# First attention: three PSUM banks for the second scores and two for the first, in place of two and three

## The chip, the cores and the metric

The kernel runs on one core of one Trainium2 chip, as one launch. The metric is the device time of that launch in microseconds; lower is better. The core has five engines with a queue of instructions each: TensorE (matmuls, written PE below, its weight loads PEld), VectorE (DVE), ScalarE (ACT), GpSimd (POOL) and SyncE (SP), which here issues DMAs.

## The reference

Four layers over x of shape 32 x 256 x 128 (batches, tokens, width), each followed by a residual addition and a layernorm without weights:

```
x = layernorm(x + attention0(x))   # 16 heads of 8, rotary embedding, softmax(q k / sqrt(8)) v, then w_out and bias
x = layernorm(x + ffn0(x))         # ternary weights, gelu, layernorm inside
x = layernorm(x + attention1(x))   # queries are the keys, heads mixed after the softmax
x = layernorm(x + ffn1(x))         # silu(gate) * up, integer weights
```

The change touches attention0 alone. There, for each of the 32 batches and 16 heads, 256 x 256 scores are computed, the maximum of each query's row is subtracted, the exponential is taken, and the result is multiplied with the values and divided by its sum.

## The kernel before

All four layers are phases of one program, written out engine by engine; `program` (L1720 on) lists what each engine does in which order, and semaphores tie the engines together. In the first attention one call of `step(i, on)` is a pass: it works on several batches at once, each at another stage. The 16 positions s = 0 to 15 of a pass are its inner loop, on every engine. `on(k)` tells whether batch i+k exists. Passes run from i = -4 to n+1 with n = 32; those from 4 to 27 are the body of a hardware loop, the others are written out.

Each score is computed twice. The *first scores* (`first_score`, L1114) are those of batch i+1: two matmuls, one for each half of 128 queries, write a 128 x 512 bank. VectorE reads that bank with one `tensor_reduce` (`max_of_head`, L967) to get the negated maximum of each row. Eight heads' maxima are turned by TensorE (`shifts_turned`, L1038), copied to SBUF by ScalarE (`shift_rows_out`) and sent by DMA into a row of the query operand, so that the *second scores* come out with the maximum already subtracted. The second scores (`second_score`, L1101) are those of batch i, with keys on the partitions. ScalarE reads their bank with one `Exp` (L912) into `probs`. `products_by_group` (L1047) multiplies four heads' `probs` with the values, after positions 3, 7, 11 and 15.

In `both_scores` (L1128) TensorE interleaves the two kinds, tile by tile: second, first, second, first. The first and second scores of one position use different rows of the array. TensorE takes its instructions in the order written, so whatever it waits for also holds up what stands behind.

Ahead of the scores of a position, `others_of_first` (L1160) puts TensorE's other work: at 2 the projection of V for batch i+1, a turn of maxima and one projection (k side) for batch i+3; at 6 two kinds of transposes (`heads_t`, `x_in`); at 10 a turn of maxima and the transposes of `o`; at 14 the output projection and the other projection (q side) for batch i+4. VectorE and ScalarE have the matching work at fixed positions among their maxima and exps: VectorE has a rotation (`rotate`, L979, 128 x 512) after the maximum of position 2 and one before that of position 15, a reciprocal before that of 6, scalings after those of 6 and 7, and an addition (y) after that of 14.

PSUM has eight banks. In the first attention the first scores have banks 0 to 2, the second scores banks 3 and 4, the products bank 5, and all other work banks 6 and 7. The banks are taken in a fixed order, and the order repeats with each pass of 16 positions:

```
s1_order = (0, 1, 2) * 4 + (0, 1) * 2     # bank of the first scores at position s
s2[s % 2]                                 # bank of the second scores at position s
```

Before the first tile of a position, `first_score` waits until the maximum that read this bank last is done (semaphore `max_done`; `s1_free`, L563, counts how many positions ago that was), and `second_score` waits on `exp_done` for the exp two positions back. With the order above the first scores wait for the maximum three positions back at positions 3 to 13, seven back at 2, and two back at 14, 15, 0 and 1.

The second attention is built by the same function with other banks: two for each kind of score, both taken in turn.

Of the kernel before, what the change touches and what calls it, by code (L numbers as in the profile page):

```python
# [9 lines left out]
ACT = mybir.ActivationFunctionType  # L10
AX = mybir.AxisListType

P = 128
D = 128
TOK = 256
TILES = TOK // P
HEADS = 16
# [16 lines left out]
RING = 8  # L34
# [46 lines left out]
def wait(eng, sem, count):  # L81

    if isinstance(count, int) and count <= 0:
        return
    eng.wait_ge(sem, count)
# [18 lines left out]
class Phase:  # L104
# [8 lines left out]
    def sem(self, name):  # L113
        self.sems[name] = self.core.sem(f"{name}_{self.name}")
        return self.sems[name]
# [23 lines left out]
def times(i, k, n):  # L139

    if isinstance(i.half, int):
        return max(0, min(n, 2 * i.half + i.odd + k + 1))
    assert i.first + i.odd + k >= 0, "no wait in a loop is for less than one"
    return i.half * 2 + (i.odd + k + 1)
# [303 lines left out]
def attention(nc, core, layer, banks, scratch, ctx, x_dram=None, before=None):  # L448
# [9 lines left out]
    n = core.n  # L458
    first = layer == 0
# [2 lines left out]
    half_heads = HEADS // 2  # L462

    b = [core.bank[k] for k in banks]
    s1, s2 = (b[0:3], b[3:5]) if first else (b[0:2], b[2:4])
    pv, m0, m1 = (b[5:6], b[6], b[7]) if first else (b[4:7], b[7], b[7])
    s1_order = (0, 1, 2) * 4 + (0, 1) * 2 if first else (0, 1) * 8
    groups = HEADS // 4
    regions = groups // 2
    slots = Slots(first)  # L470
# [3 lines left out]
    def sb(name, shape, dt=FP32):  # L474
        return ctx.enter_context(nc.sbuf_tensor(f"{name}_{layer}", shape, dt))
# [12 lines left out]
    probs = sb("probs", [P, RING, TILES, TOK])  # L488
# [42 lines left out]
    max_done = sem("max_done")  # L531
# [4 lines left out]
    exp_done = sem("exp_done")  # L536
# [23 lines left out]
    def s1_bank(s):  # L560
        return s1[s1_order[s]]

    def s1_free(b, s):  # L563

        ago = min(k for k in range(1, HEADS + 1) if s1_order[(s - k) % HEADS] == s1_order[s])
        return b.number() * HEADS + (s - ago + 1)

    banked = [h for h in range(HEADS) if h != BESIDE]
# [9 lines left out]
    def stack_rows(parity, rows=HEAD_ROWS):  # L578
        return slice(parity * TILE_ROWS, parity * TILE_ROWS + rows)
# [234 lines left out]
    def _(act):  # L814
        def shift_rows_out(b, hf):

            act.wait_ge(shifts_in_psum, b.number() * 2 + (hf + 1))

            wait(act, shifted[hf], b.number() * 16)
            act.activation(shift_rows[hf][:, :], m0[:, :].bitcast(BF16)[0:half_heads, SHIFTS_AT:SHIFTS_AT + TOK], ACT.Copy).then_inc(shift_rows_ready, 1)  # L820

        def take_heads(b, r):

            act.wait_ge(pv_done, b.number() * groups + 2 * (r + 1))
            act.activation(heads_t[b.odd][:, r, :], pv[0][:, 0:TOK], ACT.Copy).then_inc(pv_taken, 1)
# [15 lines left out]
        def norm(b, ts=range(TILES)):  # L841

            act.wait_ge(rstd_ready, b.number() + 1)
            act.wait_ge(norm_shift_ready, b.number() + 1)
            for t in ts:
                act.activation(core.x_all[:, b.number(), t, :], y_of(b)[:, t, :], ACT.Identity, scale=rstd[:, t:t + 1],
                               bias=norm_shift[:, t:t + 1]).then_inc(x_ready, 1)
# [10 lines left out]
        def second_part(b):  # L858

            act.wait_ge(rest_ready, times(b, 0, n))  # L860
            act.activation(parts[b.odd][:, 1, 0, :], rest[:, 0, :], ACT.Copy).then_inc(part1_ready, 1)

        def step(i, on):
            for s in range(HEADS):
                if not first and s == 4 and on(slots.q_ahead):
                    second_part(i.plus(slots.q_ahead))
                if first and s == slots.shifts1 and on(0):
                    shift_rows_out(i, 1)
                if s == 4 and first and on(-1):
                    take_heads(i.plus(-1), 1)  # L870
                if first and s == slots.norm and on(-2):
                    norm(i.plus(-2), (0,))
                if first and s == slots.v + 2 and on(1):
                    b = i.plus(1)
                    act.wait_ge(v_in_psum, times(i, 1, n))

                    wait(act, pv_done, times(i, -1, n) * groups)
                    act.activation(values[b.odd][:, :, :, 0:HD],
                                   m0[:, 0:TOK].rearrange("p (t h d) -> p t h d", t=TILES, d=HD),
                                   ACT.Copy).then_inc(v_taken, 1)  # L880
                if not first and s == 15 and on(slots.v_ahead):
                    act.wait_ge(v_in_psum, times(i, slots.v_ahead, n))

                    wait(act, values_ready, times(i, 1, n) * (2 * TILES))
                    act.activation(v_in[:, :, :].rearrange("p t d -> p (t d)"), m0[:, TOK:2 * TOK], ACT.Copy).then_inc(v_taken, 1)
                if s == 13 and first and on(0):
                    take_heads(i, 0)
                if s == slots.ot + (1 if first else 0) and on(-1):
                    act.wait_ge(ot_in_psum, times(i, -1, n))
                    act.activation(o_t[:, :], m1[:, 0:TOK], ACT.Copy).then_inc(ot_ready, 1)  # L890
                if s == slots.shifts0 and on(1):
                    shift_rows_out(i.plus(1), 0)
                if s == slots.xt + (1 if first else 0) and on(slots.xt_ahead):
                    b = i.plus(slots.xt_ahead)
                    act.wait_ge(xt_in_psum, times(i, slots.xt_ahead, n))

                    if first:
                        wait(act, x_v_ready, times(i, 2, n))
                        act.activation(x_t[b.odd][:, :], m0[:, 0:TOK], ACT.Copy).then_inc(xt_ready, 1)  # L899
                    else:  # L900
                        act.activation(x_t[b.odd][:, :], m1[:, 0:TOK], ACT.Identity, scale=core.cols[:, 8:9],
                                       bias=core.cols[:, 9:10]).then_inc(xt_ready, 1)
                if not first and s % 2 and on(0 if s > 4 else -1):
                    scale_head(i if s > 4 else i.plus(-1), (s - 4) % HEADS)
                if on(0):
                    act.wait_ge(s_in_psum, i.number() * HEADS + (s + 1))

                    if first and s % 4 == 0:
                        wait(act, pv_done, i.number() * groups + (s // 4 - 1))
                    if not first:  # L910
                        wait(act, pv_done, i.number() * HEADS + (s + 1 - RING))
                    act.activation(probs[:, s % RING, :, :].rearrange("p t n -> p (t n)"), s2[s % 2][:, :], ACT.Exp,  # L912
                                   scale=scale).then_inc(exp_done, 1)
                if not first and s == slots.shifts1 and on(0):
                    shift_rows_out(i, 1)
                if not first and s == slots.q and on(slots.q_ahead):
                    take_qk(i.plus(slots.q_ahead))
                if first and s == HEADS - 1 and on(-2):
                    norm(i.plus(-2), (1,))
                if not first and s == slots.norm and on(-1):  # L920
                    norm(i.plus(-1))
# [115 lines left out]
    def _(pe):  # L1037
# [63 lines left out]
        def second_score(b, s, t):  # L1101

            if t == 0:
                if s % half_heads == 0:
                    pe.wait_ge(shifted[s // half_heads], b.number() * 16 + 16)

                wait(pe, exp_done, b.number() * HEADS + (s - 1))
            rows = stack_rows(s % 2, HEAD_ROWS + 1)
            score = pe.matmul(s2[s % 2][:, t * TOK:(t + 1) * TOK], core.k_stack[b.odd][rows, s // 2, t * P:(t + 1) * P],  # L1109
                              core.q_stack[b.odd][rows, s // 2, :], start=True, stop=True)  # L1110
            if t == TILES - 1:
                score.then_inc(s_in_psum, 1)

        def first_score(b, s, t):  # L1114

            if t == 0:
                if s % half_heads == 0:
                    pe.wait_ge(stacked[s // half_heads], b.number() * (16 * reads) + 16 * reads)

                wait(pe, max_done, s1_free(b, s))  # L1120
            h = s ^ 1
            rows = stack_rows(h % 2)
            score = pe.matmul(s1_bank(s)[:, t * TOK:(t + 1) * TOK], core.q_stack[b.odd][rows, h // 2, t * P:(t + 1) * P],  # L1123
                              core.k_stack[b.odd][rows, h // 2, :], start=True, stop=True)
            if t == TILES - 1:
                score.then_inc(max_in_psum, 1)
# [758 lines left out]
```

## Time and profile before

| | |
|---|---|
| time, median of 3 runs | 1529.43 us (1526.62 to 1534.0) |
| time of the profiled execution | 1530.18 us |
| its span in the profile | 1527.9 us |
| busy share of the span: PE, PEld | 95%, 75% |
| busy share of the span: DVE, ACT, POOL | 77%, 69%, 63% |
| mean granted TensorE clock | 0.976 of full speed |
| instructions | 55309 |

The span is the time from the first to the last record of the profiled execution; the time beside it includes what lies around it. The first attention takes from about 37 us (its first scores) to about 500 us, where the feed-forward layer's work is mixed in. In a profile, busy time is the union of an engine's instructions. Matmuls are pipelined: one starts 0.1 us after another though each is 0.27 us long, so their starts say more than their durations. The list of waits names, for each idle stretch of an engine, the instruction whose semaphore came last; in a list in order of time, equal instructions in a row are merged (x16 is a count), and a gap with its releaser stands in square brackets.

### The profile page before, as it was taken

Reading aid. Unit: us, or ns where it says so; the run is one execution under the profiler, and the core shown is the slowest. Engines: PE = TensorE matmul, PEld = TensorE weight load, DVE = VectorE, ACT = ScalarE, POOL = GpSimd, SP = SyncE. Lnnn points to the kernel's source line nnn. Section 1 sums busy time; section 2 is a strip of 40 time slices with the busy share of each in tenths; the row PEclk is TensorE's granted clock in tenths of the full one; section 3 lists DMA queues with packets and bytes.
Section 4 is the critical chain, followed back from the end, with each engine's and each line's share of the span. In section 5 each row is a group of like instructions: output and inputs, shape, how many; then the busy total and the mean of one; then the engine's idle time right before and its main releaser. Section 6 shows DMA issues by size and latency. Waiting matters only on the chain. (4 is left out here: it accounts for less than half of the span.)

```text
span 1527.9 us, 55309 instructions
## 1 busy us (share of the span) xinstructions
PE 1456.4 (95%) x17642; PEld 1141.6 (75%) x17642; DVE 1180.8 (77%) x3338; ACT 1056.9 (69%) x2581; POOL 967.4 (63%) x1160
## 2 busy tenths in 40 slices
PE   5999999999999899979999999999999999998998
PEld 3445555554554499959989999999999999897997
DVE  4688888888888478878887888788878887864666
ACT  2477777777778888856777777777777777773332
POOL 4465565656554167777777877787778777852222
PEclk7699999999999999979999999999999999999999
DMA  5345454454444100122222222222222222201211
GB/s 146 105 128 135 132 140 128 132 140 126 134 131 135 34 32 33 55 74 79 82 69 90 76 79 69 90 76 80 69 90 76 80 70 85 75 23 32 65 62 52
DMA packets 174124, 133.93 MB, mean 88 GB/s; under 512 B 13787, under 2 KB 145126, under 8 KB 174054
## 3 DMA queue, kind: packets, MB, share of 16 engines
q1 hardware_dynamic: 172944, 132.37, 30.0%
q8 instruction: 40, 0.66, 0.2%
q10 hardware_dynamic: 1110, 0.66, 0.1%
q14 instruction: 30, 0.25, 0.1%
HBM read 64.82 MB, written 55.05 MB: 78 GB/s over the span
## 5 line engine op out<-in xcount | busy, mean ns | idle before, releaser
L971 DVE TENSOR_REDUCE shifts<-bank 128x2 bf16<-128x512 f32 x1024 | 682.2, 686 | 158.7 <-PE bank L1123 158.1
L912 ACT ACTIVATE probs<-bank 128x512 f32<-128x512 f32 x1024 | 579.9, 595 | 120.1 <-PE bank L1109 116.3
L1071 PE MATMUL bank<-values,probs 64*128 64x129 f32 x8192 | 577.8, 276 | 0.9 <-DVE o_even L938 0.7
L1071 PEld LDWEIGHTS bank<-values,probs 64*128 64x128 f32 x8192 | 528.8, 188 | 20.4 <-issue 4.5
L1123 PE MATMUL bank<-stack 48*128 48x256 bf16 x2048 | 373.3, 277 | 29.7 <-DVE shifts L971 24.1
L1109 PE MATMUL bank<-stack 49*128 49x256 bf16 x2048 | 373.3, 274 | 7.6 <-ACT probs L912 2.4
L715 POOL TENSOR_TENSOR values<-mix,v_in 128x1024 f32<-128x1024 f32 x128 | 302.3, 2363 | 0.0
L1109 PEld LDWEIGHTS bank<-stack 49*128 49x128 bf16 x2048 | 163.9, 95 | 139.4 <-ACT probs L912 89.7
L724 POOL TENSOR_TENSOR o_odd<-o_odd,scaled 128x256 f32<-128x256 f32 x224 | 163.5, 730 | 128.0 <-ACT scaled L838 124.3
L838 ACT ACTIVATE scaled<-bank,recips 128x128 f32<-128x128 f32 x448 | 138.6, 360 | 92.8 <-DVE recips L965 92.7
L1123 PEld LDWEIGHTS bank<-stack 48*128 48x128 bf16 x2048 | 156.2, 96 | 54.0 <-DVE shifts L971 37.8
L938 DVE SCALAR_TENSOR_TENSOR o_even<-bank,recips,o_even 128x128 f32<-128x128 f32 x448 | 136.6, 347 | 7.9
L1061 PE MATMUL bank<-probs,values 128*32 128x256 f32 x2048 | 138.8, 389 | 0.0
L965 DVE RECIPROCAL recips<-bank 128x2 f32<-128x2 f32 x512 | 84.4, 165 | 58.0 <-PE bank L1071 48.9
L740 POOL TENSOR_TENSOR shifted_var<-moments,ln_shift 128x2 f32<-128x2 f32 x64 | 12.6, 196 | 156.0 <-DVE moments L1021 145.6
L1061 PEld LDWEIGHTS bank<-probs,values 128*32 128x32 f32 x2048 | 53.8, 110 | 50.1 <-issue 28.4
L793 POOL TENSOR_TENSOR exact<-turned 128x512 f32<-128x512 f32 x32 | 40.6, 1268 | 76.2 <-DVE turned L979 71.5
L1228 PE MATMUL bank<-x_t,w_qk 128*128 128x256 f32 x256 | 76.0, 424 | 1.4 <-ACT x_t L899 1.4
L1524 PE MATMUL bank<-w_proj,h_t_f 128*128 128x129 f32 x512 | 70.2, 281 | 2.3 <-issue 1.4
L1617 POOL TENSOR_TENSOR var_f<-moments_f,ln_shift 128x2 f32<-128x2 f32 x32 | 6.2, 195 | 102.3 <-DVE moments_f L1675 102.3
L1524 PEld LDWEIGHTS bank<-w_proj,h_t_f 128*128 128x128 f32 x512 | 63.5, 191 | 5.9 <-issue 4.1
L1639 ACT ACTIVATE gate_f<-bank 128x256 f32<-128x256 f32 x96 | 36.6, 383 | 43.1 <-PE bank L1697 43.0
(165 smaller groups left out, 2176.8 us busy)
## 6 DMA issues: line engine op xcount, KB each, us to landing
stack<-score_parts SPq DMA_DIRECT2D x64, 512.0 KB, 4.2
stack<-score_parts SPq DMA_DIRECT2D x256, 96.0 KB
score_parts<-parts SPq DMA_DIRECT2D x256, 64.0 KB, 2.1
score_parts<-parts SPq DMA_DIRECT2D x128, 96.0 KB, 2.6
score_parts<-parts SPq DMA_DIRECT2D x64, 192.0 KB, 2.3
x_in_f<-x_all SPq DMA_DIRECT2D x64, 128.0 KB, 2.0
score_parts<-parts SPq DMA_DIRECT2D x64, 128.0 KB, 2.2
x_in<-in_L_attn_x SPq DMA_DIRECT2D x32, 128.0 KB, 2.1
```

Of the source, the lines that this page charges most:

```text
L715: pool.tensor_tensor(values[i.plus(1).odd][:, t, heads, 0:D], core.mix[:, heads, :], v_in[:, t, :].unsqueeze(1).broadcast_to([P, half_head ...
L724: pool.tensor_tensor(o_odd[b.odd][:, :, :], o_odd[b.odd][:, :, :], scaled[:, h // 2 % 4, :, :], op=ALU.add).then_inc(odd_added, 1)
L838: act.activation(to, pv_bank(h)[:, t * (D + 1):t * (D + 1) + D], ACT.Copy, scale=recips[:, h % 2, t:t + 1]).then_inc(scaled_ready, 1)
L912: act.activation(probs[:, s % RING, :, :].rearrange("p t n -> p (t n)"), s2[s % 2][:, :], ACT.Exp, scale=scale).then_inc(exp_done, 1)
L938: dve.scalar_tensor_tensor(o_even[b.odd][:, t, :], part, recips[:, h % 2, t:t + 1], o_even[b.odd][:, t, :], op0=ALU.mult, op1=ALU.add).the ...
L965: dve.reciprocal(recips[:, h % 2, :], sums).then_inc(recips_ready, 1)
L971: dve.tensor_reduce(shifts[:, :, hf, col], s1_bank(s)[:, :].rearrange("p (t n) -> p t n", t=TILES), op=ALU.max, axis=AX.X, negate=True).th ...
L1061: last = pe.matmul(pv[0][VW * a:VW * (a + 1), 0:TOK], values[b.odd][:, t, :, :].rearrange("p h c -> p (h c)")[:, start:start + VW], probs[ ...
L1071: return pe.matmul(pv_bank(h)[:, q * (D + 1):(q + 1) * (D + 1)], probs[rows, h % RING, t, q * P:(q + 1) * P], values[b.odd][rows, t, h, :] ...
L1109: score = pe.matmul(s2[s % 2][:, t * TOK:(t + 1) * TOK], core.k_stack[b.odd][rows, s // 2, t * P:(t + 1) * P], core.q_stack[b.odd][rows, s ...
L1123: score = pe.matmul(s1_bank(s)[:, t * TOK:(t + 1) * TOK], core.q_stack[b.odd][rows, h // 2, t * P:(t + 1) * P], core.k_stack[b.odd][rows, ...
L1524: pe.matmul(out_banks[i.odd][:, t * width:t * width + D + 1], h_t[i.odd][:, c, own], core.w0_proj[:, c, :], start=(c == 0), stop=(c == chu ...
```

## The change

The first attention's five score banks are split the other way round: banks 0 and 1 for the first scores, banks 2, 3 and 4 for the second. The order of the first scores becomes (0, 1) eight times, so each waits for the maximum two positions back. The second scores take their three banks in turn, the last position taking the second of them; they wait for the exp three positions back at positions 3 to 14, four back at 0 and 2, two back at 1 and 15. The counting function is now used for both. The second attention's banks and waits stay the same. No instruction is added, removed or moved.

```diff
-    s1, s2 = (b[0:3], b[3:5]) if first else (b[0:2], b[2:4])
+    s1, s2 = (b[0:2], b[2:5]) if first else (b[0:2], b[2:4])
     pv, m0, m1 = (b[5:6], b[6], b[7]) if first else (b[4:7], b[7], b[7])
-    s1_order = (0, 1, 2) * 4 + (0, 1) * 2 if first else (0, 1) * 8
+    s1_order = (0, 1) * 8
+    s2_order = (0, 1, 2) * 5 + (1,) if first else (0, 1) * 8
...
-    def s1_free(b, s):
-
-        ago = min(k for k in range(1, HEADS + 1) if s1_order[(s - k) % HEADS] == s1_order[s])
+    def bank_free(b, s, order=s1_order):
+
+        ago = min(k for k in range(1, HEADS + 1) if order[(s - k) % HEADS] == order[s])
         return b.number() * HEADS + (s - ago + 1)
...
-                    act.activation(probs[:, s % RING, :, :].rearrange("p t n -> p (t n)"), s2[s % 2][:, :], ACT.Exp,
+                    act.activation(probs[:, s % RING, :, :].rearrange("p t n -> p (t n)"), s2[s2_order[s]][:, :], ACT.Exp,
...
-                wait(pe, exp_done, b.number() * HEADS + (s - 1))
+                wait(pe, exp_done, bank_free(b, s, s2_order))
             rows = stack_rows(s % 2, HEAD_ROWS + 1)
-            score = pe.matmul(s2[s % 2][:, t * TOK:(t + 1) * TOK], core.k_stack[b.odd][rows, s // 2, t * P:(t + 1) * P],
+            score = pe.matmul(s2[s2_order[s]][:, t * TOK:(t + 1) * TOK], core.k_stack[b.odd][rows, s // 2, t * P:(t + 1) * P],
...
-                wait(pe, max_done, s1_free(b, s))
+                wait(pe, max_done, bank_free(b, s))
```

## Rows read from the trace of the kernel before

The pass shown runs from position 10 at 300.90 us over position 2 of the next pass (308.32) to position 8 at 315.00. L1109 are second scores, L1123 first scores, L1061 products, L971 maxima, L912 exps.

**Rows 1.** The page's part 1: busy us, share of the span, instructions.
```profile
PE 1456.4 (95%) x17642; PEld 1141.6 (75%) x17642; DVE 1180.8 (77%) x3338; ACT 1056.9 (69%) x2581; POOL 967.4 (63%) x1160
```

**Rows 2.** Stretches: busy us of PE, PEld, DVE, ACT, POOL (count), clock, DMA share, GB/s.
```profile
51.00:67.00 16.00, 15.21 (x101) 6.49 (x101) 9.47 (x17) 7.75 (x17) 7.48 (x7) 0.50 0.47 122
...
200.00:300.00 100.00, 94.43 (x1048) 50.87 (x1047) 84.15 (x177) 76.91 (x169) 57.08 (x75) 1.00 0.50 133
```

**Rows 3.** Groups by line, 150 to 450 us: busy us, mean ns, idle before.
```profile
L971 DVE TENSOR_REDUCE shifts<-bank 128x2 bf16<-128x512 f32 x325 | 211.4, 684 | 46.8 <-PE bank L1123 46.8
L912 ACT ACTIVATE probs<-bank 128x512 f32<-128x512 f32 x325 | 184.7, 596 | 59.3 <-PE bank L1109 58.6
```

**Rows 4.** Waits, 150 to 450 us: us in total, times, longest.
```profile
PEld bank L1109 <- ACT probs L912: 53.2, 163, 0.4
...
PEld bank L1123 <- DVE shifts L971: 19.5, 20, 1.0
...
PE bank L1123 <- DVE shifts L971: 13.9, 20, 0.7
```

**Rows 5.** TensorE in order of time, one pass: start us, us, what, count.
```profile
300.90 0.44 PE L1210 MATMUL bank<-ident,o 128*128 128x128 f32 x2
301.31 0.28 PE L1109 MATMUL bank<-stack 49*128 49x256 bf16 x1
...
301.80 0.28 PE L1109 MATMUL bank<-stack 49*128 49x256 bf16 x1
...
302.20 1.07 PE L1061 MATMUL bank<-probs,values 128*32 128x256 f32 x16
303.20 0.28 PE L1109 MATMUL bank<-stack 49*128 49x256 bf16 x1
...
308.00 0.28 PE L1123 MATMUL bank<-stack 48*128 48x256 bf16 x1 [0.69 <-DVE shifts L971]
...
308.32 0.71 PE L1168 MATMUL bank<-w_v,x_v 128*128 128x128 f32 x4
...
310.23 0.28 PE L1109 MATMUL bank<-stack 49*128 49x256 bf16 x1
...
310.77 1.07 PE L1061 MATMUL bank<-probs,values 128*32 128x256 f32 x16
311.77 0.28 PE L1109 MATMUL bank<-stack 49*128 49x256 bf16 x1
...
312.84 0.38 PE L1198 MATMUL bank<-ident,x_in 128*128 128x128 f32 x2
313.15 0.28 PE L1109 MATMUL bank<-stack 49*128 49x256 bf16 x1
...
313.60 0.28 PE L1109 MATMUL bank<-stack 49*128 49x256 bf16 x1
...
315.00 0.28 PE L1109 MATMUL bank<-stack 49*128 49x256 bf16 x1
```

**Rows 6.** VectorE in order of time, same pass and columns.
```profile
307.25 0.69 DVE L971 TENSOR_REDUCE shifts<-bank 128x2 bf16<-128x512 f32 x1
...
310.69 0.70 DVE L971 TENSOR_REDUCE shifts<-bank 128x2 bf16<-128x512 f32 x1 [1.03 <-PE bank L1123]
311.30 0.68 DVE L979 TENSOR_TENSOR turned<-bank,rope 128x512 f32<-128x512 f32 x1
311.89 1.88 DVE L971 TENSOR_REDUCE shifts<-bank 128x2 bf16<-128x512 f32 x3
...
313.95 0.63 DVE L971 TENSOR_REDUCE shifts<-bank 128x2 bf16<-128x512 f32 x1
```

**Rows 7.** ScalarE in order of time, same pass and columns.
```profile
312.45 1.72 ACT L912 ACTIVATE probs<-bank 128x512 f32<-128x512 f32 x3
```

**Rows 8.** TensorE in order of time, V projection eleven passes on.
```profile
471.64 0.71 PE L1168 MATMUL bank<-w_v,x_v 128*128 128x128 f32 x4
```

## The prediction

> **What bounds the kernel now.** I began with the page's busy shares [rows 1]. They name TensorE at 95%, but for matmuls such a share counts overlapping instructions, so it can't say that TensorE sets the pace. The change touches only the first attention, so I then read that stretch alone [rows 2]: of 100 us VectorE is busy 84, ScalarE 77, and the granted clock is 1.00, the upper level of 2.4 GHz. No engine is full, so the pace is set by a loop of waits. The projection for V starts once per pass, at 308.32 and again at 471.64, eleven passes later [rows 5, 8]: 14.85 us per pass.
>
> Next, the price of one head. A row maximum on VectorE lasts 0.69 us, an exp on ScalarE 0.60 [rows 3]. Back to back their starts are 0.60 and about 0.49 apart: three maxima take 1.88 us, and three exps 1.72, the third waiting a little [rows 6, 7]. TensorE needs about 0.23 for both scores of a head: the two heads 2 and 3 and the switch to other work take 0.54, from 310.23 to 310.77 [rows 5]. So the scores are cheap for TensorE. It stalls because a bank is not yet read.
>
> Then who it waits for [rows 4]. In 300 us, the second scores' weight loads stood 53.2 us behind ScalarE, in 163 places; the first scores stood 19.5 us (loads) and 13.9 us (matmuls) behind VectorE. Taken at face value that asks for a third bank at ScalarE. The order of time says otherwise. At 303.20, where such a wait is booked, TensorE has just finished the products that began at 302.20, and a group of products takes 1.00 wherever it is followed by scores, as from 310.77 to 311.77 [rows 5]. It was working, and the load had nothing to wait for. I count the starts of matmuls instead. Real stalls of one pass, S1(s), S2(s) being the scores at position s, M(s) and E(s) the maximum and the exp that empty them:
> 1. S1(1) waits for M(15), which ends at 307.25 + 0.69 = 307.94; TensorE resumes at 308.00, 0.06 later. The row's gap of 0.69 begins where the matmul before it ended; that lasts 0.27, and the next could have started with it, so the stall is 0.96 [rows 5, 6].
> 2. S2(7) starts 0.45 after S2(6), against 0.23: 0.22 for E(5), which starts about 312.94 and ends 0.60 later [rows 5, 7].
> 3. S2(11) starts 0.49 after S2(10): 0.26 for E(9).
> 4. S2(10) comes about 0.1 late behind E(8): the two transposes at 300.90 need some 0.3 (as the two at 312.84, after which scores start at 313.15), and it starts at 301.31.
>
> **What the change does to each stall.** No instruction is added or moved. Only which earlier reader a score waits for changes. First scores at positions 3 to 13 wait for M(s-2) in place of M(s-3) (position 2 too, from seven back). Second scores wait for E(s-3) or E(s-4), and for E(s-2) at 1 and 15 alone. At 14, 15, 0 and 1 the first scores already wait for two back. So stall 1 stays: M(15) is behind M(14), the addition to y and a rotation on VectorE, a chain that begins with TensorE's own scores at position 14. Stalls 2 to 4 go, worth 0.22 + 0.26 + 0.10 = 0.58 per pass. What is late next, walked on the clock of this pass:
>
> - **Position 5.** M(2) starts 0.46 after the scores of position 2 (310.23, 310.69), then comes the rotation, then M(3) at 311.89 [rows 6]. M(3) ends at 311.89 + 0.69 = 312.58, and S1(5) may go at 312.64. TensorE gets there at 311.77 + 0.23 = 312.00. New stall 0.63. The transposes, with which heads_t and x_in are turned, queue behind it.
> - **Positions 6 and 7.** Position 6 moves from 313.15 to 313.78, and 7 comes 0.23 later at 314.01. E(4) is long done for S2(7), and M(5) ends about 313.78 (the three maxima from 311.89 end at 313.77). So 7 is 0.41 late against 313.60: of 0.63, ScalarE's stall gives 0.22 back. Position 8 comes at 315.00 + 0.41 = 315.41.
> - **Position 9.** M(6) can't start before 313.78 + 0.46 + some 0.03, 314.27 in place of 313.95. M(7) follows after M(6) at 0.60 and a scaling at about 0.18: 315.05, ending 315.74, so S1(9) goes at 315.80. TensorE arrives at 315.41 + 0.23 = 315.64: stall 0.16, now 0.57 late.
> - **Positions 10 and 11.** Without stall 4, position 10 comes 0.47 late. M(8) starts at 315.41 + 0.46 = 315.87, M(9) 0.60 after it, ending 317.16, so S1(11) goes at 317.22. One tile and the switch (0.31) later the products start at 317.53. Before, they started at 302.20 + 14.85 = 317.05. **+0.48.**
> - **Positions 12 to 1.** M(10) and M(11) end at 317.8 and 318.4; the scores that want them come at 318.53 and 318.76. From 14 on the waits are those of before. Everything shifts by 0.48, stall 1 keeps its size.
>
> So 0.63 + 0.16 and some 0.33 at position 11 come in, 0.58 go, and a little is lost to rounding: I take +0.47 per pass. DMAs: none is added, and the shift rows' queue is moved as a whole with its pass.
>
> **The sum.** Passes 1 to 28 have this shape: 28 x 0.47 = 13.2. Passes 29 and 30 have no rotation at position 2 (it is for batch i+3), so M(3) is not late: nothing. Passes -1 and 0 run while the clock is still low (0.50, the level of 1.2 GHz, from 51 to 67 us [rows 2]); first scores alone wait there for VectorE, about one maximum (0.69) more each before the projections: 1.4. The second attention gets the same banks and waits as before: nothing. 1530.2 for the profiled execution, plus 14.6, is 1544.8; the median of the three runs is 0.75 lower, so I say **1544.5**. A measurement of this kernel can tell about 0.5% (7.6 us) from no change.
>
> The bounds per pass: if none of ScalarE's stalls gave anything back, 0.63 + 0.16 + 0.33 = 1.12; if VectorE never held a bank, -0.58. I take 0.47 because each end needs M(3) or E(5) elsewhere than the rows have them.
>
> The Trainium skill speaks on both sides. Its page "Perfetto Trace Analysis", section "Identifying the Most-Contended Engine", ranks VectorE and ScalarE by occupancy and would have the fuller one served first: that is VectorE, from which the change takes a bank, as the trace here bears out. The same page of the Trainium skill, section "Optimization Strategy", says that consistent bubbles can mean too little PSUM; by that, the 163 waits for ScalarE would call for exactly this bank, and the time would come out as in rival A below.
>
> **Rivals.**
> - **A, faster.** The waits booked to ScalarE [rows 4] are real throughout, and M(3) is in time. Place: S1(5). It decides if M(3) ends before 311.94, 0.64 earlier than the row has it. Price: stalls 2 to 4 go and nothing comes, 28 x -0.58 = -16: 1514. For it: the size of the booked waits. Against: the rotation between M(2) and M(3) is in every pass. 6%, with smaller gains.
> - **B, absorbed.** The delay at position 5 is swallowed later, above all by stall 1, so that +0.1 to +0.2 per pass is left: 28 times that, plus 1.4, gives 1534 to 1537. For it: 0.96 us of slack stands there. Against: that stall's chain starts from TensorE's position 14 and moves with it. 9%.
> - **C, no effect.** TensorE's 95% is its true limit and stalls only change places: 1530. Against: 0.96 us of nothing at S1(1) in each pass. 5%.
> - **D, the full price.** VectorE becomes the loop: each of its waits adds (1.12 per pass) and ScalarE's savings don't show, as E(5) and E(8) are late behind the delayed scores. 28 x 1.12 = 31, plus 1.4: 1563. For it: two banks give a round trip of 0.69 + 0.06 + 0.46 = 1.21 for two maxima, exactly their 0.60 each, without slack. Against: outside positions 5, 9 and 11 TensorE's other work comes later than the maxima. 10%.
> - **The forecast**, +0.3 to +0.7 per pass, 1540 to 1551: 70%.
>
> **Numbers.** Slower by over 0.5%: forecast and D, 0.80. Within: B and C, 0.14. Faster: A, 0.06. The range leaves out A, C and most of D: 1534 to 1555, down into B, and up to the forecast's edge with a third of the way to D.
>
> **What would show it.** In the profile after: a pass of 15.3 us by the starts of the V projection; no gap before S2(7) and S2(11), and instead one of about 0.6 before S1(5), 0.2 before S1(9) and 0.3 before S1(11), with VectorE as releaser; waits of first scores for VectorE up by about a us per pass; the 0.69 gap at S1(1) unchanged; the second attention as long as before. The forecast is wrong if the pass is 14.3, if S1(5) starts within 0.3 of S1(4), or if the gap at S1(1) shrinks by what is lost at position 5.

## The result and the profile after

The changed kernel takes 1543.88 us (median of 6 runs, 1540.23 to 1544.83), against 1528.84 for the kernel before (median of 6, 1526.62 to 1534.0): a ratio of 1.0091, 95% interval 1.0073 to 1.011. It is slower by 15 us, and the interval is clear of no change and above the 0.5% named in the prediction. The profiled execution took 1544.36 us, its span 1542.1.

First the length of a pass. Below is TensorE in order of time in the changed kernel, one pass from one V projection (L1169, here one line later than before) to the next; columns as in [rows 5].

```profile
301.98 0.71 PE L1169 MATMUL bank<-w_v,x_v 128*128 128x128 f32 x4
...
303.89 0.28 PE L1110 MATMUL bank<-stack 49*128 49x256 bf16 x1
...
305.44 0.28 PE L1110 MATMUL bank<-stack 49*128 49x256 bf16 x1
...
305.67 0.27 PE L1110 MATMUL bank<-stack 49*128 49x256 bf16 x1
306.30 0.28 PE L1124 MATMUL bank<-stack 48*128 48x256 bf16 x1 [0.36 <-DVE shifts L972]
...
307.43 0.28 PE L1110 MATMUL bank<-stack 49*128 49x256 bf16 x1
...
307.66 0.27 PE L1110 MATMUL bank<-stack 49*128 49x256 bf16 x1
...
307.97 1.07 PE L1062 MATMUL bank<-probs,values 128*32 128x256 f32 x16
308.98 0.28 PE L1110 MATMUL bank<-stack 49*128 49x256 bf16 x1
...
309.21 0.27 PE L1110 MATMUL bank<-stack 49*128 49x256 bf16 x1
309.44 0.28 PE L1124 MATMUL bank<-stack 48*128 48x256 bf16 x1
...
309.97 0.44 PE L1211 MATMUL bank<-ident,o 128*128 128x128 f32 x2
310.34 0.28 PE L1110 MATMUL bank<-stack 49*128 49x256 bf16 x1
...
310.57 0.27 PE L1110 MATMUL bank<-stack 49*128 49x256 bf16 x1
310.84 0.28 PE L1124 MATMUL bank<-stack 48*128 48x256 bf16 x1
...
311.16 1.07 PE L1062 MATMUL bank<-probs,values 128*32 128x256 f32 x16
...
316.95 0.28 PE L1124 MATMUL bank<-stack 48*128 48x256 bf16 x1 [0.69 <-DVE shifts L972]
...
317.27 0.71 PE L1169 MATMUL bank<-w_v,x_v 128*128 128x128 f32 x4
```

A pass is now 317.27 - 301.98 = 15.29 us, against 14.85 [rows 5, 8]. Counted from the V projection: position 2 starts at 1.91, as before (310.23 - 308.32). Position 4 is also where it was, 3.46. Then the first scores of position 5 start at 4.32, with the new gap of 0.36 and VectorE as releaser, and everything behind is late: position 6 at 5.45 (before 4.83), 8 at 7.00 (6.68), 10 at 8.36 (7.84), the products at 9.18 (8.73, which is 302.20 + 14.85 - 308.32). The gap of 0.69 before S1(1), at 316.95, is the one of [rows 5]. The row's 0.36 is the idle time after the last matmul; counted from starts, as in the prediction, S1(5) comes 0.63 after S2(5), at which TensorE had arrived (306.30 - 305.67), S1(9) 0.23 after S2(9) and S1(11) 0.27 after S2(11).

The waits of 150 to 450 us, in the columns of [rows 4]:

```profile
PEld bank L1124 <- DVE shifts L972: 41.6, 79, 1.0
PEld bank L1110 <- ACT probs L913: 33.9, 98, 0.4
...
PE bank L1124 <- DVE shifts L972: 20.4, 39, 0.7
```

The first scores' loads wait 41.6 us for VectorE, in 79 places, where it was 19.5 us in 20 [rows 4]: four per pass (positions 1, 5, 9 and 11) in place of one. The waits booked to ScalarE fell from 53.2 to 33.9. VectorE around position 5, with the columns of [rows 6]:

```profile
304.35 0.70 DVE L972 TENSOR_REDUCE shifts<-bank 128x2 bf16<-128x512 f32 x1 [1.03 <-PE bank L1124]
304.96 0.68 DVE L980 TENSOR_TENSOR turned<-bank,rope 128x512 f32<-128x512 f32 x1
305.56 1.89 DVE L972 TENSOR_REDUCE shifts<-bank 128x2 bf16<-128x512 f32 x3
...
307.89 0.70 DVE L972 TENSOR_REDUCE shifts<-bank 128x2 bf16<-128x512 f32 x1 [0.19 <-PE bank L1124]
...
309.30 0.28 DVE L954 TENSOR_TENSOR o<-bank,recips 128x128 f32<-128x128 f32 x1
309.49 2.60 DVE L972 TENSOR_REDUCE shifts<-bank 128x2 bf16<-128x512 f32 x4
```

M(2) starts 0.46 after the scores of position 2, the rotation follows, M(3) starts at 305.56, and S1(5) goes at 306.30, 0.05 after M(3)'s 0.69 are over. The stretch from 200 to 300 us as in [rows 2]:

```profile
200.00:300.00 100.00, 93.67 (x1037) 49.66 (x1039) 83.39 (x170) 75.80 (x166) 58.40 (x72) 1.00 0.47 126
```

VectorE went from 84.2 to 83.4 and ScalarE from 76.9 to 75.8, at the same granted clock of 1.00 (2.4 GHz): neither reader became busier. The shares fell by 1% and the pass grew by 3%; busy time per pass therefore rose a little, which fits readings that no longer follow one another at once and are booked with their full length (0.69 in place of 0.60 for a maximum).

### The profile page after: what moved, and what is told of

Read it like the earlier page. It is cut to its first block and busy times, and to the rows that moved or that the text cites. A ratio compares the mean times of both kernels' runs of the same rounds, so it can differ in the third digit from the quotient of the medians.

```text
span 1542.1 us, 55297 instructions
## 1 busy us (share of the span) xinstructions
PE 1466.1 (95%) x17642; PEld 1144.9 (74%) x17642; DVE 1188.2 (77%) x3338; ACT 1062.1 (69%) x2581; POOL 967.0 (63%) x1160
## 5 line engine op out<-in xcount | busy, mean ns | idle before, releaser
L1124 PE MATMUL bank<-stack 48*128 48x256 bf16 x2048 | 379.3, 277 | 41.7 <-DVE shifts L972 36.4
L1110 PE MATMUL bank<-stack 49*128 49x256 bf16 x2048 | 377.3, 274 | 2.7 <-ACT probs L913 1.3
```

The costliest lines, as they stand in the source:

```text
L1110: score = pe.matmul(s2[s2_order[s]][:, t * TOK:(t + 1) * TOK], core.k_stack[b.odd][rows, s // 2, t * P:(t + 1) * P], core.q_stack[b.odd][r ...
```

## The experiments

Pass lengths below are differences of successive starts of the V projection, as above; unlike a run's time they repeat to 0.01 or 0.02 us within the hardware loop. The exceptions are e2 and e5, which alternate between two values, and the first or second looped pass of e2, e5, e7 and e9, which is 0.02 to 0.19 longer. The kernel before, run beside the experiments, has medians of 1529.6 to 1530.4. Where the table says "one run", the time is too coarse for small differences (the kernel before spreads over 1524.6 to 1535.2), and the pass decides.

| kernel | pass, us | time, us |
|---|---|---|
| before | 14.85 | 1528.84 |
| the change | 15.29 | 1543.88 |
| e1: two and two banks | 15.29 | 1545.03 |
| e2: before, S1(5) waits two back | 15.17 to 15.22 | 1541.8 (one run) |
| e3: before, S1(9), S1(11) wait two back | 14.94 | 1531.74 (one run) |
| e7: before, half of each exp | 14.35 | 1511.62 (one run) |
| e4: change, rotation behind M(3) | 15.08 | 1537.37 (one run) |
| e5: before, rotation behind M(3) | 14.87 to 14.90 | 1534.23 (one run) |
| e6: before, loop written out | 14.61 | 1521.5 |
| e8: before, q rotation behind M(15) | 14.52 | 1521.23 (one run) |
| e9: before, rotation and y behind M(15) | 14.19 | 1509.29 |
| e10: change, rotation and y behind M(15) | 14.62 | 1528.34 (one run) |
| e11: e9 with the loop written out | 14.02 | 1505.21 |

**Is the third bank of the second scores worth anything?** e1 takes it away again.

```diff
-    s2_order = (0, 1, 2) * 5 + (1,) if first else (0, 1) * 8
+    s2_order = (0, 1) * 8
```

> The changed kernel with the second scores on two banks again, so that the first attention has two and two and one bank lies idle. Theory: the third bank of the second scores buys nothing once the first scores have two, because TensorE now comes to the second scores after the exps: E(9) would end about 8.5 us after the V projection, S1(11) waits until 8.8 anyway. Pass 15.29 us (starts of the V projection), as with the change, time 1542 to 1546. Rival (the third bank gives back the 0.58 us per pass of ScalarE's stalls, as the prediction booked it): pass 15.6 to 15.9, time 1552 to 1560.

Measured: pass 15.29, time 1545.03 (four runs), ratio to before 1.0108 (1.0086 to 1.013). The pass is that of the change to 0.01 us. The rival, that the bank gives back 0.58, is out. TensorE of this kernel at positions 9 and 11:

```profile
308.95 0.28 PE L1110 MATMUL bank<-stack 49*128 49x256 bf16 x1
309.12 0.28 PE L1124 MATMUL bank<-stack 48*128 48x256 bf16 x1
...
310.30 0.28 PE L1110 MATMUL bank<-stack 49*128 49x256 bf16 x1
310.51 0.28 PE L1124 MATMUL bank<-stack 48*128 48x256 bf16 x1
```

S2(9) and S2(11) still stall a little (308.95 and 310.30), but each time the first scores behind them wait longer, until 309.12 and 310.51. TensorE's order is fixed, so only the later of the two releases counts.

**Which positions pay?** e2 and e3 keep the banks of before and make single waits stricter.

```diff
         ago = min(k for k in range(1, HEADS + 1) if s1_order[(s - k) % HEADS] == s1_order[s])
+        if first and s in (5,):
+            ago = 2
```

This is e2; e3 has `(9, 11)` in place of `(5,)`.

> The kernel before, with its banks, but the first scores of position 5 alone wait two maxima back. Theory: S1(5) goes 4.32 us after the V projection in place of 3.69; of the 0.63, E(5)'s stall and the lag of S1(7) behind S2(7) give back 0.31, and ScalarE's later stalls move with it: pass 15.17 (+0.32). Rival (position 5 carries the whole change): pass 15.29. Rival (stalls of ScalarE at 10 and 11 absorb it): pass 14.9.

> The kernel before, but the first scores of positions 9 and 11 wait two maxima back. Theory: S1(9) goes 7.12 us after the V projection, S1(11) 8.51 in place of 8.41: pass 14.95 (+0.10). With the run for position 5 the two make up the whole 0.44. Rival (position 5 carries the whole change): 14.85.

Measured: +0.32 to +0.37 for position 5 (its looped passes alternate between 15.17 to 15.18 and 15.20 to 15.22, 15.19 on average), +0.09 for positions 9 and 11. Together 0.41 to 0.46, the 0.44 of the change. Both single-cause rivals are out. The gap at S1(5) in e2 is the one of the changed kernel; S1(5) at 317.30 is 4.32 after the V projection:

```profile
312.98 0.71 PE L1170 MATMUL bank<-w_v,x_v 128*128 128x128 f32 x4
...
317.30 0.28 PE L1125 MATMUL bank<-stack 48*128 48x256 bf16 x1 [0.36 <-DVE shifts L973]
```

**What were ScalarE's stalls worth before?** e7 shortens each exp of the first attention to 256 of 512 columns (the second half of the keys gets probability zero, from one memset ahead of the first pass).

```diff
-                    act.activation(probs[:, s % RING, :, :].rearrange("p t n -> p (t n)"), s2[s % 2][:, :], ACT.Exp,
-                                   scale=scale).then_inc(exp_done, 1)
+                    if first:
+                        act.activation(probs[:, s % RING, 0, :], s2[s % 2][:, 0:TOK], ACT.Exp, scale=scale).then_inc(exp_done, 1)
...
+            dve.memset(probs[:, :, 1, :], 0.0).then_inc(ones_ready, 1)
```

> The kernel before, but in the first attention each exp takes only 256 of the 512 columns, so the probabilities of the second half of the keys stay zero: this part of the computation is left out, to take ScalarE out of the loop of waits. It shows what the stalls behind ScalarE cost before. Theory (counted from starts: 0.58 us per pass): pass 14.3 to 14.4, by when VectorE's maxima hold TensorE at positions 10 and 11. Rival (the waits booked to ScalarE, 53.2 us in 300, are real): pass 12.3 to 13. Rival (ScalarE is hidden): 14.85.

Measured: pass 14.35, 0.50 less. The booked waits of this kernel and the engine's groups, 150 to 450 us:

```profile
ACT probs L913 <- PE bank L1113: 104.3, 168, 1.0
...
PEld bank L1113 <- ACT probs L913: 32.5, 104, 0.4
...
PEld bank L1127 <- DVE shifts L974: 20.5, 21, 1.0
...
PEld bank L1047 <- DVE shifts L974: 8.4, 21, 0.4
```

```profile
L913 ACT ACTIVATE probs<-bank 128x256 f32<-128x256 f32 x336 | 120.5, 386 | 104.3 <-PE bank L1113 104.3
```

An exp takes 0.386 us now and ScalarE waits 104 us for TensorE, so it holds nobody up. Still 32.5 us in 104 places stand as weight loads that waited for ScalarE. These are loads behind groups of products and behind the transposes: TensorE was busy, and the list names the semaphore that came last. Of the 53.2 us booked before, about 0.5 us per pass, some 10 us in 300, was real.

The 0.50 is a net figure, and the starts give its parts. S2(7) and S2(11) now follow one head (0.23) behind S2(6) and S2(10), which takes off 0.22 and 0.26; S2(10) comes 0.04 earlier behind its transposes. With the stalls goes a lag of S1 behind S2 at positions 7 and 11, 0.09 and 0.08, of which e6 below tells more. That is 0.69. About 0.19 comes back, because the turn of maxima ahead of position 10 (L1047 here) now waits longer for VectorE: 8.4 us in 21 places, where the kernel before has

```profile
PEld bank L1043 <- DVE shifts L971: 4.4, 21, 0.2
```

**Is it the rotation that makes M(3) late?** e4 takes the changed kernel and puts the rotation of position 2 behind M(3); e5 does the same to the kernel before.

```diff
-                if first and s == slots.k and on(slots.k_ahead):
+                if first and s == slots.k + 1 and on(slots.k_ahead):
                     rotate(i, 1, slots.k_ahead)
```

> The changed kernel with VectorE's rotation of position 2 put behind M(3) in place of M(2). Theory: S1(5) waits for M(3), and M(3) waits for the rotation; so the stall before S1(5) goes from 0.63 to about 0.05 us. The transposes of position 6 then wait for the rotation (bank 7), and M(5), M(7), M(9) hold S1(7), S1(9), S1(11) a little: pass 15.08 us (-0.21). Rival (the rotation does not matter, two banks are simply too few): 15.29.

> Control: the kernel before with the same move of the rotation. Theory: its first scores wait three back, so M(3) is early either way; the transposes of position 6 wait 0.29 us for the rotation, which E(5)'s stall at position 7 hides: pass 14.85, as before. Rival (the move is a gain of its own): pass below 14.75.

Measured: e4 15.08, the forecast figure; e5 14.87 to 14.90 (forecast 14.85, so a slight loss and no gain of its own). The rotation's place matters only where the first scores have two banks. In e4 VectorE does M(2) and M(3) in one go, and then the rotation:

```profile
313.40 1.30 DVE L972 TENSOR_REDUCE shifts<-bank 128x2 bf16<-128x512 f32 x2 [1.03 <-PE bank L1124]
314.61 0.68 DVE L980 TENSOR_TENSOR turned<-bank,rope 128x512 f32<-128x512 f32 x1
```

Half of the 0.44 goes with it: S1(5) waits 0.04 in place of 0.63. The rest stays with two banks at a round trip of two maxima. M(5) and M(7) hold S1(7) and S1(9) by 0.15 and 0.08, and M(9) holds S1(11) by 0.37:

```profile
319.31 0.27 PE L1110 MATMUL bank<-stack 49*128 49x256 bf16 x1
319.68 0.28 PE L1124 MATMUL bank<-stack 48*128 48x256 bf16 x1
```

**Why did written-out passes take 14.62 and looped ones 14.85 before?** e6 writes the loop out.

```diff
-    attn0.loop(4)
+    attn0.at(*range(4, n - 4))
```

> The kernel before with the hardware loop over passes 4 to 27 of the first attention written out, so that all waits are for constants. In the trace of before, passes 1 to 3, written out, take 14.62 us and looped ones 14.85; in the loop S1 starts 0.09 us after S2 wherever S2 had stalled behind ScalarE. Theory: after a stall TensorE's queue must still work out the register for the wait of the first scores. Pass 14.62 throughout, 24 x 0.23 = 5.5 us less: about 1523. Rival (the difference is the norm or other work that early passes lack): looped passes keep 14.85, no gain, or a loss from fetching more instructions.

Measured: 14.61 in all passes, time 1521.5 (four runs), ratio 0.9944 (0.9922 to 0.9965). Around position 7, TensorE:

```profile
306.72 0.28 PE L1109 MATMUL bank<-stack 49*128 49x256 bf16 x1
306.72 0.28 PE L1123 MATMUL bank<-stack 48*128 48x256 bf16 x1
...
307.04 1.07 PE L1061 MATMUL bank<-probs,values 128*32 128x256 f32 x16
308.05 0.28 PE L1109 MATMUL bank<-stack 49*128 49x256 bf16 x1
```

S2(7) and S1(7) start together here, and position 8 follows S2(7) after 1.33. In the kernel before it takes 1.40, from 313.60 to 315.00 [rows 5], and the first scores start behind the second at 7 and at 11 (316.65, 316.73):

```profile
313.69 0.28 PE L1123 MATMUL bank<-stack 48*128 48x256 bf16 x1
...
316.65 0.28 PE L1109 MATMUL bank<-stack 49*128 49x256 bf16 x1
316.73 0.28 PE L1123 MATMUL bank<-stack 48*128 48x256 bf16 x1
```

That is 0.07 and 0.08 of the 0.24. The third part comes by way of ScalarE. In the kernel before E(8) starts 0.51 behind S2(8) (315.51 and 315.00), in e6 0.42 (308.47 and 308.05):

```profile
315.51 1.08 ACT L912 ACTIVATE probs<-bank 128x512 f32<-128x512 f32 x2 [0.57 <-PE bank L1109]
```

```profile
308.47 1.08 ACT L912 ACTIVATE probs<-bank 128x512 f32<-128x512 f32 x2 [0.41 <-PE bank L1109]
```

E(9) follows E(8), and S2(11), which waits for E(9), comes 0.49 behind S2(10) before and 0.40 in e6. E(8) stands behind two waits in a row, for its scores and for a group of products. All three losses are gone where all waits are for constants. This fits a register that a queue works out behind a stalled wait; the profile does not show that step, so the cause is narrowed to the loop and not shown further.

**Is stall 1 to be had, and does the bank split look better then?** Neither split touches it. e8 moves the rotation of position 15 behind M(15) (the first part of the edit), e9 the addition to y as well, e10 is e9's edit on the changed kernel, e11 is e9 with the loop written out.

```diff
+                if on(1):
+                    max_of_head(i.plus(1), s)
                 if first and s == slots.q + 1 and on(slots.q_ahead):
                     rotate(i, 0, slots.q_ahead)
-                if on(1):
-                    max_of_head(i.plus(1), s)
...
-                if s == slots.out and on(-1):
+                if s == slots.out + (1 if first else 0) and on(-1):
                     b = i.plus(-1)
```

> The kernel before with VectorE's other rotation, of position 15, put behind M(15). Neither bank split touches this stall (0.96 us before S1(1)). Theory: M(15) ends 0.60 earlier, S1(1) goes 0.60 earlier, then the V projection waits for the rotation (bank 6): pass 14.52 us (-0.33), time about 1520. Rival (the stall comes from TensorE's late position 14 and stays): 14.85.

> The kernel before with the rotation and the addition to y both behind M(15). Theory: M(15) follows M(14) at once, S1(1) finds its bank free about when TensorE arrives (stall 0.05 in place of 0.96), and the V projection waits for the rotation, 0.6 after S1(1): pass 14.20 us (-0.65), time about 1510. Rival (the later norm work of VectorE runs into M(0) to M(2) and gives it back): pass 14.4 to 14.5, as with the rotation alone.

> The changed kernel (two and three banks) with the same two moves. Theory: the price of the bank split sits at positions 5 to 11 and does not depend on the stall at 1: pass 14.20 + 0.44 = 14.64 us, time about 1525. Rival (with VectorE's stall gone, ScalarE is what is left, and its third bank pays): pass at or below that of the other run.

> The kernel before with both moves and the loop of the first attention written out. Theory: the two gains add: pass 14.20 - 0.23 = 13.97 us, time 1502 to 1507. Rival (the moves remove the stalls at which the loop's registers cost time): pass 14.2.

Measured: e8 14.52. e9 14.19, 1509.29 us, ratio 0.9854 (0.9824 to 0.9884). e10 14.62, so the split still costs 0.43 with the stall gone, and the rival that it would then pay is out. e11 14.02, 1505.21 us, ratio 0.9835 (0.981 to 0.9859): the loop gave 0.17 and not the 0.23 forecast, and by time alone e11 and e9 can't be told apart. VectorE and TensorE of e9 around the end of a pass:

```profile
322.61 1.29 DVE L971 TENSOR_REDUCE shifts<-bank 128x2 bf16<-128x512 f32 x2 [0.76 <-PE bank L1123]
323.81 0.68 DVE L979 TENSOR_TENSOR turned<-bank,rope 128x512 f32<-128x512 f32 x1
```

```profile
323.96 0.28 PE L1123 MATMUL bank<-stack 48*128 48x256 bf16 x1
...
324.55 0.71 PE L1168 MATMUL bank<-w_v,x_v 128*128 128x128 f32 x4 [0.20 <-DVE turned L979]
```

M(14) and M(15) now follow each other, S1(1) goes at 323.96, and what TensorE waits for there is the rotation, 0.20 before the V projection. e9 and e11 beat both kernels.

## Why the prediction was right, and where it was off

- **The stall at position 5** came as walked: 4.32 us after the V projection (predicted 312.64 - 308.32 = 4.32), behind M(2), the rotation and M(3). e2 and e4 show it to be the cause of most of the loss.
- **Positions 9 and 11**: walked to 7.48 and 8.90 (315.80 and 317.22), measured 7.46 and 8.86. e3 shows them as a price of their own, 0.09. The three new stalls are 0.63, 0.23 and 0.27, where the prediction books 0.63, 0.16 and some 0.33: 1.13 against 1.12.
- **Positions 12 to 1** shift as a block and stall 1 keeps its 0.69 gap. Rival B, that this slack absorbs the delay, fell: its chain begins with TensorE, and moved along.
- **The pass**: 0.47 predicted, 0.44 measured. The term that was too large is the delay at position 8, 0.41 in the walk and 0.32 in the trace. I gave back 0.22 for the stall of S2(7), and overlooked that S1(7) starts another 0.09 behind S2(7) in the looped passes before, which goes with the stall. e6 shows that lag to belong to the loop. Only 0.04 of this 0.09 reaches the pass: VectorE has a scaling ahead of M(8), which starts at 7.51 (309.49 - 301.98) where the walk has 7.55.
- **What goes** is not 0.58. Stall 4 was misread: the two transposes of `o` need 0.37 with nobody to wait for (309.97 to 310.34), not the 0.3 of the two of `x_in`, so 0.04 of their 0.41 before was a stall and not 0.10. The stalls are 0.22 + 0.26 + 0.04 = 0.52. The two lags of S1 behind S2, 0.09 and 0.08, go too, and 1.13 - 0.52 - 0.17 = 0.44. By the prediction's own terms the pass grows by 1.12 - 0.58 = 0.54; the 0.07 down to 0.47 that it calls rounding is in the main the lag at position 11, which its walk contained and its list of stalls did not.
- **The written-out passes**. In passes 1 to 3, written out, the change cost more: they took 14.62 and take 15.28 to 15.29, +0.67, since there was no loop loss to give back. The sum took 0.47 for these too.
- **The sum** came out for passes 1 on: from the V projection of pass 1 to that of pass 30 the change added 439.16 - 425.98 = 13.2 us, for 28 x 0.47 = 13.2. Its smaller terms were off both ways: 24 looped passes gave 10.5, three written-out ones 2.0, pass 28 gave 0.5 and pass 29, predicted as nothing, 0.15. That these meet the 13.2 so closely is luck. From there to the end nothing changed (1030.5 and 1030.3 us).
- **The 1.4 us for passes -1 and 0** can't be judged. The V projection of pass 1 came 1.2 us later, but over the other kernels, most of them with edits that hardly touch those passes, the two passes took from 29.0 to 34.3 us. The forecast of 1544.5 for a median of 1543.88 owes some of its closeness to this. Its last step is also loose: 1544.8 less 0.75 is 1544.05.
- **Bookings of second scores' waits**: the reading that most of them were no stalls held. e7 gains 0.50 us per pass net from stalls of 0.52 (counted: 0.58). In the changed kernel the stalls did go, but e1 shows that it was not the third bank that removed them. With VectorE late they vanish on two banks too.
- **Rivals A, C and D** fell: the pass grew (A, C), and by far less than 1.12 (D), because the 0.69 of stalls and lags went. The waits of first scores for VectorE rose by about 1.5 us per pass (41.6 + 20.4 in 19.6 passes against 19.5 + 13.9 in 20.2), where the prediction looked for about 1; the list books some stalls twice, as a load's and as a matmul's. As for the rules of the Trainium skill, page "Perfetto Trace Analysis": the one in "Identifying the Most-Contended Engine", to serve the engine with the highest occupancy, agrees with these runs (VectorE, 84 against 77). The one in "Optimization Strategy", that consistent bubbles can mean too little PSUM, did not hold for the bubbles booked to ScalarE: e1 and the change have the same pass.

## What to carry to other kernels

Where one in-order engine feeds two readers from two rings of buffers, a buffer is worth what it does to the later of the two releases; walk one period by starts, position by position, before moving one. A wait in a list is only a stall if the starts show it: behind a group of products the list named ScalarE for work that TensorE was doing. And before trading banks, look at what stands between the readings on the fuller engine: moving two instructions behind a maximum was worth 21 us here (1530.4 to 1509.3), more than the banks either way.

## What the hardware showed that I had not expected

- In the hardware loop a pass cost 0.24 us more than in written-out code (14.85 against 14.61 us). The starts put it at three places where an engine goes on after a wait: S1(7) and S1(11) behind stalled second scores on TensorE (0.07 and 0.08) and E(8) on ScalarE (0.09). Between e9 and e11 the same places lose 0.26 up to the products of position 11 (8.73 and 8.47 us after the V projection), and 0.09 of it comes back by the end of the pass. The written-out program runs fewer instructions (52926 against 55309), and the larger code cost nothing that these runs show.
- The start is the noisy part. The granted clock in the first two passes differs between executions, though e6 edits neither of them: in the kernel before it is 0.50 (1.2 GHz) from 60 to 68 us, in e6 1.00 (2.4 GHz):

```profile
60.00:68.00 8.00, 8.00 (x64) 3.08 (x61) 4.91 (x9) 4.72 (x11) 5.94 (x6) 0.50 0.35 93
```

```profile
60.00:68.00 8.00, 7.31 (x93) 3.37 (x82) 7.24 (x13) 5.90 (x13) 5.50 (x6) 1.00 0.40 109
```

In the profiled execution of e6 the two passes took 28.98 us against 33.71, a gain of 4.7 us beside the 5.7 of the 24 looped passes, so the whole of its 8 us can't be put down to the loop. In e6 the clock rose about 57 us into the span (0.79 from 56 to 58 us, 1.00 from 58 on), in the kernel before about 68 us. From 48 to 56 us, with the clock at 0.50 in both, TensorE was equally busy (7.03 us of 8 in each); what raised it earlier stays open.
